# Attention seams in a three-layer hybrid block: order of denominators, first weighting, eviction and reciprocal

## Chip, cores and metric

The kernel runs on one core of a Trainium2 chip. The metric is the device time of one execution in microseconds, as the median of several runs. The core has five engines that work side by side and wait for one another with semaphores: TensorE (PE, matrix products), VectorE (DVE), ScalarE (ACT), GpSimd (POOL) and SyncE (SP, which issues DMAs). Products land in PSUM, eight banks of 128 partitions x 512 fp32.

## What is computed

Input x is (4, 1024, 512) in fp32. Four layers follow one another, each on the layer norm of x and added to x: attention, a top-2 mixture of experts, a state-space mixer, and the experts again. The change is in the attention alone:

```python
kqv = x @ Wqkv + bqkv                              # 16 heads of 32
scores = jnp.einsum('bsnh,btnh->bnst', k, q) / math.sqrt(HEAD_SIZE)
scores = jnp.triu(scores) + -10000.0 * jnp.tril(ones, k=-1)
attn = jax.nn.softmax(scores, axis=2)
out = jnp.einsum('bnkq,bknh->bqnh', attn, v)
out = out.reshape(b, s, NUM_HEADS * HEAD_SIZE)
return out @ Wo + bo
```

## The kernel before

A loop runs over the 4 batches. In the attention of one batch the 16 heads go by pairs: p = 0 to 7, in four groups g of two pairs (hf = 0 and 1). Even pairs are hf 0, odd ones hf 1. During an even pair TensorE also projects queries and keys of the next group (L741 to L743, four parts of 12 matmuls, into PSUM bank 7); the last group has no next one, so pair 6 has no projection. The loop over the groups is split into first, middle and last part, and each engine has its own hand-written order of work; what follows is that order, and each engine keeps strictly to its own.

The scores of a pair are formed twice. Row tiles (`scores_a`, L864 and the mask L867, ten tiles "a" 0 to 9) give the maxima, which VectorE takes (`maximum`, L1586). They are formed one pair ahead. The maxima are turned (`turn_maxima`, L874), cast by ScalarE (L1246) and sent by two DMAs from ScalarE's queue (L1249) into an extra row of QS. Column tiles (`scores_b`, L886 and L889, twelve units u, units 0 to 3 over the first 512 queries and 4 to 11 over the last 512) carry that row, and are then exponentiated by ScalarE into the four buffers of PR (`exponential`, L1263). Three banks of two rotate for all these score tiles, so that a tile waits for the reader of the one three tiles back. Unit 4's scores are the first that wait for the second half of the row of maxima.

On PR three things are done. `weigh` (L906, six times a pair, k = 0 to 5, eight groups of products each) multiplies with the values into bank 6; it waits for the two exponentials of its units, k = 0 also until both halves of the previous pair's outputs are evicted, k = 2 until the first half of its own is. GpSimd adds the units up into `acc` (`sums`, a copy L1922 and ten additions L1913); it starts a pair when the previous pair's denominators are formed, and an exponential waits for GpSimd's reader of its buffer. `denominators` (L916) sums `acc` over partitions with a matrix of ones into bank 7, for the previous pair, right behind the first weighting.

VectorE evicts the outputs (`take`, L1598 to L1601, one half of the queries at a time). ScalarE copies the denominators to `rec` (`take_denominators`, L1270), VectorE inverts them in two halves (`invert`, L1608) and multiplies the outputs (`scale`, L1618, two operations). `rec` is one buffer, so the copy waits for the scaling of the pair before. On VectorE the end of a pair is: first reciprocal of the previous pair, second eviction of this one, second reciprocal, scaling. In an even pair the next thing is `group_lo` (L1622), then the maxima of tiles 0 and 1 and the first eviction of the next pair. The projection of the next group waits on TensorE until the denominators in bank 7 have been copied (den_act). "Seam" means the stretch between the last weighting of a pair and the third weighting of the next.

Of the kernel before, what the change touches and what calls it, by code (L numbers as in the profile page):

```python
# [148 lines left out]
def hybrid_layer(nc, x, Wqkv, bqkv, Wo, bo, W_in, conv_w, conv_b, z_bias, Dskip, W_out,  # L149
                 Wr, br, Wd, bd, Wu, bu, out):  # L150
    with ExitStack() as ctx:
# [108 lines left out]
        pj_lo = signal("pj_lo", 4)  # L260
# [449 lines left out]
        def _(pe):  # L710
# [100 lines left out]
            with pe.Fori(0, NB) as b:  # L811
# [64 lines left out]
                def scores_b(slots, p, q, slot, occ, job):  # L876

                    u = job[1] % UNITS
                    c, s, t0, n = span(u)
                    if s == 0:  # L880
                        pe.wait_ge(s_mrow[slot][c], occ * 32 + 32)
                    slot_free(slots, p, job)
                    bank = slots.bank[job]
                    diag = s * P >= c * HB
                    for hh in range(2):
                        i = pe.matmul(ps[:, bank + hh, 0:n], KS[slot][:, hh, s * P:(s + 1) * P],  # L886
                                      QS[slot][:, hh, t0:t0 + n], start=True, stop=not diag)
                        if diag:
                            i = pe.matmul(ps[:, bank + hh, 0:P], identb[:, :], mask_st[:, :], start=False, stop=True)  # L889
                    i.then_inc(st_pe.sem, 1)  # L890

                def weigh(p, hf, k):

                    ex.wait(pe, p, 2 * k + 2)
                    if k == 0:
                        o_copied.wait(pe, p, 0)
                        vg_done.wait(pe, p, 1)
                    elif k == 2:
                        o_copied.wait(pe, p, 1)
                    for j in range(2):  # L900
                        u = 2 * k + j
                        c, s, t0, n = span(u)
                        at = t0 - c * HB
                        for hh in range(2):
                            h, o = (2 * hf + hh) * HS, j * 64 + hh * HS
                            i = pe.matmul(ps[o:o + HS, 6, at:at + n], VG[:, s, h:h + HS],  # L906
                                          PR[:, u % 4, hh, 0:n], start=(k in (0, 2)), stop=(k in (1, 5)))
                    i.then_inc(pv.sem, 1)

                def denominators(p):  # L910

                    summed.wait(pe, p, 10)
                    for c in range(2):
                        for hh in range(2):
                            o = c * 64 + hh * HS
                            i = pe.matmul(ps[o:o + HS, 7, :], ones[:, 0:HS], acc[:, c, hh, :], start=True, stop=True)  # L916
                    i.then_inc(den_pe.sem, 1)
# [13 lines left out]
                def attend(g, hf, first, last):  # L931
                    p, occ = b * 8 + g * 2 + hf, b * 4 + g
                    close = last and hf == 1
                    slots = SLOTS_CLOSE if close else SLOTS_BODY
                    for k in range(PAIRED):
                        for job in units_of(k):
                            scores_b(slots, p, p, hf, occ, job)
                        weigh(p, hf, k)
                        if k == 0 and not (first and hf == 0):
                            if hf == 1 and not first:  # L940
                                pj_lo.wait(pe, b * 4 + g, 4)
                            denominators(p - 1)
                        if not close:
                            for job in AT[k]:
                                if job[0] == "t":
                                    turn_maxima(slots, p, job[1])
                                else:
                                    scores_a(slots, p, 1 - hf, occ + hf, job[1])
                        if hf == 0 and not last and 1 <= k <= 4:
                            if k == 1 and not first:  # L950
                                den_act.wait(pe, p - 1, 1)
                            project(g + 1, k - 1)
                    if not close:
                        for job in TAIL:
                            if job[0] == "t":
                                turn_maxima(slots, p, job[1])
                            else:
                                scores_b(slots, p, p + 1, 1 - hf, occ + hf, job)

                for part in range(3):  # L960
                    with (pe.Fori(1, GROUPS - 1) if part == 1 else ExitStack()) as i_:
                        g = i_ if part == 1 else (0 if part == 0 else GROUPS - 1)
# [197 lines left out]
        def _(act):  # L1160
# [58 lines left out]
            with act.Fori(0, NB) as b:  # L1219
# [58 lines left out]
                def attend(g, hf, first, last):  # L1278
                    p, occ = b * 8 + g * 2 + hf, b * 4 + g
                    close = last and hf == 1  # L1280
                    slots = SLOTS_CLOSE if close else SLOTS_BODY
                    head = first and hf == 0
                    for u in range(UNITS):
                        exponential(slots if u >= 2 else SLOTS_BODY, ("b", u if u >= 2 else UNITS + u), p, u, head)
                        if u == 1:
                            maxima(SLOTS_BODY, p, 1, hf, None if head else occ - 1 + hf)
                            if hf == 0 and not last:
                                group_hi(b * 4 + g + 1)
                        if u == 3 and not head:
                            take_denominators(p - 1, first and hf == 1)  # L1290
                        if u == 9 and not close:
                            maxima(slots, p + 1, 0, 1 - hf, occ)
                        if hf == 0 and not last and u in (5, 7, 9, 11):
                            project_hi(g + 1, (u - 5) // 2, False)

                for part in range(3):
                    with (act.Fori(1, GROUPS - 1) if part == 1 else ExitStack()) as i_:
                        g = i_ if part == 1 else (0 if part == 0 else GROUPS - 1)
# [114 lines left out]
        def _(dve):  # L1413
# [137 lines left out]
            with dve.Fori(0, NB) as b:  # L1551
# [22 lines left out]
                def project_lo(g, ch, first):  # L1574
                    w, c = ch // 2, ch % 2
                    cols = slice(c * HB, (c + 1) * HB)
                    pj_hi.wait(dve, b * 4 + g, ch + 1)
                    dve.scalar_tensor_tensor(EV[w][1][:, cols], ps[:, 4 + ch if first else 7, :],
                                             bqk[:, w * GROUPS:w * GROUPS + 1] if first else bqk[:, bass.ds(g + w * GROUPS, 1)],
                                             EV[w][0][:, cols].bitcast(F32), ALU.add, ALU.subtract).then_inc(pj_lo.sem, 1)  # L1580
# [9 lines left out]
                def take(p, hf, c, first=False):  # L1590

                    pv.wait(dve, p, 2 if c == 0 else PAIRED)
                    if c == 0 and not first:
                        o_scaled.wait(dve, p - 2, 2)
                    rows_ = slice(c * 64, (c + 1) * 64)
                    f = P if c == 0 else 0
                    if f:
                        dve.tensor_copy(OS[rows_, hf, 0:f], ps[0:64, 6, 0:f])  # L1598
                    dve.tensor_copy(OS[rows_, hf, f:HB], ps[64:128, 6, f:HB]).then_inc(s_half, 1)
                    dve.wait_ge(s_half, p * 2 + (c + 1))  # L1600
                    dve.tensor_tensor(OS[rows_, hf, f:HB], ps[0:64, 6, f:HB], OS[rows_, hf, f:HB], ALU.add).then_inc(o_copied.sem, 1)  # L1601
# [27 lines left out]
                def attend(g, hf, first, last):  # L1629
                    p = b * 8 + g * 2 + hf  # L1630
                    close = last and hf == 1
                    head = first and hf == 0
                    if hf == 0 and not last:
                        group_lo(b * 4 + g + 1)
                    for k in range(1, 5):
                        if not close:
                            for kind, i in AT[k]:
                                if kind == "a":
                                    maximum(SLOTS_BODY, p + 1, i)
                        if k == 1:  # L1640
                            take(p, hf, 0, first)
                        if hf == 0 and not last:
                            project_lo(g + 1, k - 1, False)
                    if not head:
                        invert(p - 1, 0)
                    take(p, hf, 1)
                    if not head:
                        invert(p - 1, 1)
                        scale(p - 1, g if hf == 1 else g - 1, 1 - hf)

                for part in range(3):
                    with (dve.Fori(1, GROUPS - 1) if part == 1 else ExitStack()) as i_:
                        g = i_ if part == 1 else (0 if part == 0 else GROUPS - 1)
# [379 lines left out]
```

## Time and profile before

| | |
|---|---|
| median of 3 runs | 3432.42 us (3430.91 to 3434.16) |
| the profiled execution | 3431.01 us, its span 3429.4 us |
| busy in the span | PE 89%, weight loads 62%, DVE 64%, POOL 35%, ACT 32% |
| mean granted TensorE clock | 0.901 of full speed |
| attention of a batch | from about 187 to 440 us in the first, four times in the span |

The granted clock has two levels, 2.4 GHz (1.00) and 1.2 GHz (0.50); a number between is a mean over a stretch. In the rows, a line of a timeline gives the start in us from the start of the span, the duration of what is merged in it, the engine, line and operation, what it writes and reads, how many, and in square brackets how long the engine had been idle and what ended that. A row of the windows gives a stretch, its length in us, the busy us and number of instructions of PE, PEld, DVE, ACT and POOL in it, the mean granted clock, the busy share of the DMA engines and GB/s. GpSimd's `acc` has the name win_raw there, since it lies in the same memory. The name of TensorE's sequencer or weight load beside it is PEld, and ACTq is ScalarE's sequencer, which issues DMAs.

### The profile page before, as it was taken

Reading aid. Unit: us, or ns where it says so; the run is one execution under the profiler, and the core shown is the slowest. Engines: PE = TensorE matmul, PEld = TensorE weight load, DVE = VectorE, ACT = ScalarE, POOL = GpSimd, SP = SyncE. Lnnn points to the kernel's source line nnn. Section 1 sums busy time; section 2 is a strip of 40 time slices with the busy share of each in tenths; the row PEclk is TensorE's granted clock in tenths of the full one; section 3 lists DMA queues with packets and bytes.
Section 4 is the critical chain, followed back from the end, with each engine's and each line's share of the span. In section 5 each row is a group of like instructions: output and inputs, shape, how many; then the busy total and the mean of one; then the engine's idle time right before and its main releaser. Section 6 shows DMA issues by size and latency. Waiting matters only on the chain.

```text
span 3429.4 us, 59553 instructions
## 1 busy us (share of the span) xinstructions
PE 3043.2 (89%) x19524; PEld 2123.4 (62%) x19524; DVE 2210.9 (64%) x3101; ACT 1104.4 (32%) x1792; POOL 1217.3 (35%) x1341
## 2 busy tenths in 40 slices
PE   3598889999789888999978888899996998899998
PEld 3455457777555446777755444677774554477775
DVE  1356577777645657777764666777764565677776
ACT  1133314444113323344312332343421333144441
POOL 3346511333135541233213553133322455113331
PEclk7779899999879889999988888999998888899998
DMA  7421102111122111111122220111113211021111
GB/s 236 146 55 44 37 19 62 50 48 43 59 69 62 44 25 44 51 48 45 32 81 68 51 48 19 50 43 49 42 42 92 58 44 37 19 62 48 47 46 47
DMA packets 160075, 189.81 MB, mean 55 GB/s; under 512 B 43835, under 2 KB 103867, under 8 KB 158075
## 3 DMA queue, kind: packets, MB, share of 16 engines
q1 hardware_dynamic: 154974, 173.47, 18.2%
q0 software_dynamic: 2720, 10.49, 0.8%
q10 hardware_dynamic: 2176, 3.41, 0.4%
q8 instruction: 94, 1.54, 0.2%
q14 instruction: 111, 0.90, 0.1%
HBM read 104.90 MB, written 23.36 MB: 37 GB/s over the span
## 4 chain that ended last, share of the span: by engine, by line
PE 71%; DVE 10%; issue 5%; POOL 4%; DMA 3%; ACT 2%; SPq 2%; ACTq 1%; POOLq 0%; DVEq 0%
PE ps L741 13%; PE ps L743 12%; PE ps L742 12%; PE ps L864 5%; PE ps L906 5%; PE ps L1084 4%; PE ps L969 3%; POOL win_raw L1913 3%; PE ps L886 3%; PE ps L1070 2%; PE ps L786 2%; PE ps L1130 2%; DVE LM L1713 2%; PE ps L1093 2%; PE ps L751 1%
## 5 line engine op out<-in xcount | busy, mean ns | idle before, releaser
L741 PE MATMUL ps<-uh,win 128*128 128x512 f32 x1536 | 631.3, 411 | 3.5 <-POOL win L1874 2.8
L743 PE MATMUL ps<-uh,win 128*128 128x512 f32 x1536 | 606.7, 395 | 0.0
L742 PE MATMUL ps<-ul,win 128*128 128x512 f32 x1536 | 604.6, 394 | 0.0
L1586 DVE TENSOR_REDUCE mneg<-ps 128x1 f32<-128x640 f32 (+7 forms) x512 | 356.8, 750 | 312.9 <-PE ps L867 311.2
L1913 POOL TENSOR_TENSOR win_raw<-win_raw,PR 128x1024 f32<-128x1024 f32 (+3 forms) x256 | 419.5, 1639 | 191.7 <-ACT PR L1263 130.8
L1263 ACT ACTIVATE PR<-ps 128x1024 f32<-128x1024 f32 (+3 forms) x384 | 292.4, 808 | 357.9 <-PE ps L889 244.5
L1977 POOL TENSOR_SCALAR_AFFINE_SELECT LM<-LM 128x512 f32<-128x512 f32 x256 | 209.6, 830 | 492.4 <-ACT LM L1374 492.4
L741 PEld LDWEIGHTS ps<-uh,win 128*128 128x128 f32 x1536 | 292.3, 190 | 75.7 <-issue 9.5
L864 PE MATMUL ps<-KS,QS 96*128 96x512 f32 (+3 forms) x768 | 278.9, 476 | 67.2 <-DMA KS<-EV 37.2
L743 PEld LDWEIGHTS ps<-uh,win 128*128 128x128 f32 x1536 | 291.7, 190 | 65.9
L1737 DVE TENSOR_TENSOR LM<-ps,LM 128x512 f32<-128x512 f32 x256 | 170.1, 685 | 246.1 <-PE ps L1084 199.5
L742 PEld LDWEIGHTS ps<-ul,win 128*128 128x128 f32 x1536 | 292.8, 191 | 55.1
L886 PE MATMUL ps<-QS,KS 97*128 97x512 f32 (+3 forms) x768 | 272.1, 446 | 28.4 <-ACT PR L1263 21.7
L906 PE MATMUL ps<-PR,VG 128*32 128x512 f32 (+3 forms) x1536 | 219.6, 613 | 56.1 <-DVE OS L1601 52.1
L864 PEld LDWEIGHTS ps<-KS,QS 96*128 96x128 f32 x768 | 166.9, 250 | 143.4 <-issue 57.3
L1725 DVE SCALAR_TENSOR_TENSOR Ct<-ps,cpt,Ct 128x1023 f32<-128x1023 f32 (+2 forms) x192 | 245.5, 1279 | 15.8 <-ACT Ct L1364 11.3
L1725 DVE SCALAR_TENSOR_TENSOR Bt<-ps,cpt,Bt 128x1023 f32<-128x1023 f32 (+2 forms) x192 | 243.4, 1267 | 0.9 <-ACT Bt L1364 0.6
L886 PEld LDWEIGHTS ps<-QS,KS 97*128 97x128 f32 x768 | 163.8, 221 | 108.4 <-issue 53.1
L1184 ACT CAST uh<-ps 128x512 fp32r<-128x512 f32 x128 | 74.0, 588 | 455.7 <-PE ps L751 455.7
L1374 ACT ACTIVATE LM<-ps 128x512 f32<-128x512 f32 x256 | 147.5, 602 | 127.5 <-PE ps L1070 127.5
L1870 POOL TENSOR_TENSOR rstd<-veps,halfs 128x4 f32<-128x4 f32 x32 | 34.4, 1074 | 432.3 <-DVE veps L1447 432.3
L1084 PE MATMUL ps<-Ct,Bt 64*128 64x128 f32 x2048 | 154.2, 292 | 6.1 <-DVE Ct L1725 5.2
(224 smaller groups left out, 5384.4 us busy)
## 6 DMA issues: line engine op xcount, KB each, us to landing
raw<-in_t SPq DMA_DIRECT2D x128, 256.0 KB, 2.7
QS<-EV SPq DMA_DIRECT2D x192, 128.0 KB, 2.3
KS<-EV SPq DMA_DIRECT2D x168, 128.0 KB, 2.4
X<-in_L_attn_b_W_in_dram SPq DMA_DIRECT2D x10, 1024.0 KB, 7.6
in_t<-tiles POOLq DMA_DIRECT2D x10, 1024.0 KB, 7.9
win_raw<-in_L_attn_a_Wqkv_dram SPq DMA_DIRECT2D x34, 256.0 KB, 3.5
X<-in_L_attn_a_x_dram SPq DMA_DIRECT2D x32, 256.0 KB, 4.3
win_raw<-in_t SPq DMA_DIRECT2D x32, 256.0 KB, 2.7
```

The lines of the kernel that those rows point to most:

```text
L741: pe.matmul(dst, hi_l, hi_r, start=first, stop=False)
L742: pe.matmul(dst, hi_l, lo_r, start=False, stop=False)
L743: return pe.matmul(dst, lo_l, hi_r, start=False, stop=last)
L864: w = pe.matmul(ps[:, b0, col:col + m], QS[slot][0:STACK, hh, t * P:(t + 1) * P], KS[slot][0:STACK, hh, c:c + m], start=True, stop=not diag)
L886: i = pe.matmul(ps[:, bank + hh, 0:n], KS[slot][:, hh, s * P:(s + 1) * P], QS[slot][:, hh, t0:t0 + n], start=True, stop=not diag)
L906: i = pe.matmul(ps[o:o + HS, 6, at:at + n], VG[:, s, h:h + HS], PR[:, u % 4, hh, 0:n], start=(k in (0, 2)), stop=(k in (1, 5)))
L1084: i = pe.matmul(ps[:, 5 + h, k * P:(k + 1) * P], Bt[hs, par, tok], Ct[hs, par, tok], start=True, stop=True)
L1263: act.activation(PR[:, u % 4, :, 0:n], ps[:, bank:bank + 2, 0:n], ACT.Exp, scale=SCALE).then_inc(ex.sem, 1)
L1586: m = dve.tensor_reduce(mneg[:, t // HALF, hh, t % HALF:t % HALF + 1], wide(slots.bank["a", i])[:, at:at + (t + 1) * P], AX.X, ALU.max, ne ...
L1725: dve.scalar_tensor_tensor(dst[:, par, k:L], wide(2 * w)[:, 0:L - k], cpt[:, par, w, at:at + 1], dst[:, par, k:L], ALU.mult, ALU.add).then ...
L1913: return pool.tensor_tensor(dst, a, c, ALU.add)
L1977: pool.affine_select(out=v, in_=v, compare_op=ALU.is_ge, fill=0.0, base=0, pattern=[[0, 4], [1, P]], channel_multiplier=-1).then_inc(sel_p ...
```

## The change

Three moves, in the three engines' orders. On TensorE the denominators of the previous pair go ahead of the first weighting instead of behind it. In odd pairs with a projection before them they now wait until that last projection is evicted (before, the wait named the group before, since the weighting's own wait covered it). On ScalarE the copy of the denominators goes behind the exponential of unit 5 instead of unit 3. On VectorE the second eviction goes ahead of both reciprocals instead of between them. No operation is added or taken away.

```diff
                     for k in range(PAIRED):
                         for job in units_of(k):
                             scores_b(slots, p, p, hf, occ, job)
+                        if k == 0 and not (first and hf == 0):
+                            if hf == 1 and not last:
+                                pj_lo.wait(pe, b * 4 + g + 1, 4)
+                            denominators(p - 1)
                         weigh(p, hf, k)
-                        if k == 0 and not (first and hf == 0):
-                            if hf == 1 and not first:
-                                pj_lo.wait(pe, b * 4 + g, 4)
-                            denominators(p - 1)
                         if not close:
@@ -1286,7 +1286,7 @@
-                        if u == 3 and not head:
+                        if u == 5 and not head:
                             take_denominators(p - 1, first and hf == 1)
@@ -1641,10 +1641,9 @@
+                    take(p, hf, 1)
                     if not head:
                         invert(p - 1, 0)
-                    take(p, hf, 1)
-                    if not head:
                         invert(p - 1, 1)
                         scale(p - 1, g if hf == 1 else g - 1, 1 - hf)
```

## Rows read from the trace of the kernel before

**Rows 1.** Part 1 of the page, busy us of each engine:

```profile
PE 3043.2 (89%) x19524; PEld 2123.4 (62%) x19524; DVE 2210.9 (64%) x3101; ACT 1104.4 (32%) x1792; POOL 1217.3 (35%) x1341
```

**Rows 2.** Waits of the whole span: who for whom, us, times, longest:

```profile
ACT PR L1263 <- POOL win_raw L1913: 54.9, 35, 2.8
...
PE ps L906 <- DVE OS L1601: 52.1, 40, 2.0
```

**Rows 3.** Timeline of PE, seam before pair 3, first batch:

```profile
287.05 1.05 PE L906 MATMUL ps<-PR,VG 128*32 128x512 f32 x8 [0.87 <-DVE OS L1601]
287.74 1.23 PE L916 MATMUL ps<-win_raw,ones 128*32 128x512 f32 x8
289.06 1.19 PE L886 MATMUL ps<-QS,KS 97*128 97x512 f32 x4
...
293.17 0.50 PE L864 MATMUL ps<-KS,QS 96*128 96x512 f32 x1 [1.36 <-ACT PR L1263]
...
297.11 1.93 PE L906 MATMUL ps<-PR,VG 128*32 128x512 f32 x8 [1.77 <-DVE OS L1601]
```

**Rows 4.** Timeline of DVE, the same stretch:

```profile
283.07 0.75 DVE L1578 SCALAR_TENSOR_TENSOR EV<-ps,bqk,EV 128x512 fp32r<-128x512 f32 x1 [1.87 <-ACT EV L1237]
283.74 1.74 DVE L1608 RECIPROCAL rec<-rec 128x256 f32<-128x256 f32 x1
...
288.88 1.49 DVE L1618 TENSOR_TENSOR OT<-OS,rec 64x512 f32 x2 [0.18 <-DVE rec L1608]
291.84 1.35 DVE L1586 TENSOR_REDUCE mneg<-ps 128x1 f32<-128x512 f32 x3 [1.46 <-PE ps L867]
294.26 1.35 DVE L1586 TENSOR_REDUCE mneg<-ps 128x1 f32<-128x512 f32 x3 [1.07 <-PE ps L867]
```

**Rows 5.** Timelines of ACT and then of POOL, the same stretch:

```profile
285.85 1.27 ACTq L1249 DMA_DIRECT2D QS<-mrows  x2
...
290.41 0.59 ACT L1270 COPY rec<-ps 128x512 f32<-128x512 f32 x1 [2.15 <-DVE OT L1618]
292.09 1.94 ACT L1263 ACTIVATE PR<-ps 128x1024 f32<-128x1024 f32 x2 [1.09 <-POOL win_raw L1913]
...
279.47 0.74 POOL L1913 TENSOR_TENSOR win_raw<-win_raw,PR 128x256 f32<-128x256 f32 x1 [0.34 <-POOL win_raw L1913]
...
289.33 0.50 POOL L1922 COPY win_raw<-PR 128x256 f32<-128x256 f32 x1 [5.63 <-PE ps L916]
290.01 2.04 POOL L1913 TENSOR_TENSOR win_raw<-PR 128x768 f32<-128x768 f32 x1 [0.18 <-POOL win_raw L1922]
```

**Rows 6.** Timeline of PE, seam before pair 2:

```profile
251.26 1.92 PE L906 MATMUL ps<-PR,VG 128*32 128x512 f32 x8 [1.04 <-DVE OS L1601]
...
258.96 0.49 PE L864 MATMUL ps<-KS,QS 96*128 96x512 f32 x1 [1.72 <-ACT PR L1263]
```

**Rows 7.** Timelines of ACT's queue and of PE, seam before pair 1:

```profile
220.83 1.26 ACTq L1249 DMA_DIRECT2D QS<-mrows  x2
...
224.03 1.18 PE L886 MATMUL ps<-QS,KS 97*128 97x512 f32 x4 [1.03 <-DMA QS<-mrows]
```

**Rows 8.** Windows, ready to ready: pairs 1 (two), 3, 6, 2 and 4:

```profile
221.09:250.22 29.13, 25.28 (x139) 12.78 (x138) 14.56 (x21) 10.22 (x15) 18.11 (x12) 0.82 0.30 72
...
2707.34:2735.25 27.91, 24.02 (x139) 12.47 (x138) 14.56 (x21) 10.22 (x15) 18.13 (x12) 0.88 0.32 77
...
286.18:316.98 30.80, 26.05 (x139) 13.22 (x138) 18.64 (x26) 10.33 (x15) 18.42 (x12) 0.78 0.29 71
...
2869.93:2900.80 30.87, 26.03 (x139) 13.24 (x138) 18.80 (x26) 10.33 (x15) 17.77 (x11) 0.78 0.08 18
...
250.22:286.18 35.96, 32.65 (x186) 19.75 (x186) 22.95 (x31) 13.65 (x20) 18.77 (x12) 0.95 0.20 45
...
2804.75:2839.09 34.34, 31.26 (x186) 19.43 (x186) 24.37 (x31) 13.64 (x20) 19.17 (x12) 1.00 0.20 46
```

**Rows 9.** Timeline of DVE at the end of the first batch's attention:

```profile
437.02 2.36 DVE L1618 TENSOR_TENSOR OT<-OS,rec 64x512 f32<-64x512 f32 x2
```

## The prediction

> **What bounds the kernel now.** I read the busy table first: TensorE works 89% of the span [rows 1], so the other engines matter only where it waits for them. The list of waits comes next. It shows TensorE waiting for the evicted outputs 52.1 us in 40 places, and ScalarE's exponentials waiting for GpSimd's sums 54.9 us in 35 places [rows 2]. The third view is the timeline of one seam, that between head pairs 2 and 3 of the first batch (pairs numbered 0 to 7 in each batch). Four things are to be seen there.
>
> - The first weighting of pair 3 starts at 287.05 after 0.87 us of waiting for L1601, and TensorE was ready at 286.18 [rows 3]. VectorE could have begun the eviction at 283.82, but ran the first half of the reciprocal from 283.74 to 285.48 [rows 4]. This is the queue order that the change turns round.
> - The denominators (L916) stand behind that weighting: 287.74 to 288.97 [rows 3]. GpSimd has had its last sum done since 280.21, and sits idle 5.63 us for the denominators before it copies the next pair's first tile at 289.33 [rows 5].
> - The exponential of unit 4 reuses a buffer of PR that GpSimd's second operation (290.01 to 292.05) reads; it starts at 292.09. The second row-score tile on TensorE (L864 at 293.17) waits 1.36 us for it [rows 3, 5].
> - The third weighting (297.11) waits 1.77 us for the half eviction, which stands behind the maxima of both first tiles (291.84 and 294.26) [rows 3, 4].
>
> So each seam has a wait at the first weighting and one at L864: 1.04 and 1.72 in the seam before pair 2 [rows 6], 0.87 and 1.36 here. The first kind is there in 24 seams (before pairs 2 to 7 of four batches; pair 1 has none), the second weighting wait in 16 pairs (1, 3, 5, 6): together the 40 of [rows 2].
>
> **The change, part by part.**
>
> *Denominators ahead of the weighting.* Same eight matmul passes, 1.23 us [rows 3]. They now run from 286.18 in time that TensorE waited. They need GpSimd's last sum: done 5.97 us before [rows 5]. In odd pairs the wait on the last projection's eviction now asks for the group just projected; behind it on TensorE would stand the denominators and everything after. That eviction ends at 283.82, 2.36 us before [rows 4]. I cost both waits at nothing; if the cover were gone, each us past 286.18 would be a us for TensorE. The denominators end at about 287.4 rather than 288.97, nearly 1.6 us earlier (0.7 for the order, 0.87 for the wait), so GpSimd starts at 287.75, its second operation ends at 290.5, and the exponential of unit 4 ends at 291.5.
>
> *Outputs evicted ahead of the reciprocal.* Two reciprocals of about 1.75 us now follow the eviction. The eviction ends at 285.25, before TensorE is ready: the 0.87 us goes. The scaling still ends near 290.4, since VectorE was never idle from 283.07 to the start of it but for 0.2 us [rows 4]; nothing behind it moves.
>
> *What is late next, odd pairs and pair 6.* Unit 4's scores need the row of maxima that ScalarE sends by DMA. In pair 1, with no wait ahead, they start 1.94 us after the second issue ended at 222.09, and TensorE waits 1.03 us for it [rows 7]. In pair 3 the issues end at 287.12 [rows 5] and the scores start at 289.06 [rows 3], the same 1.94. So this transfer is a bound already, and the 0.87 us turns into a wait for it. The gain comes at L864: ready at 291.81 and released by 291.5, so its 1.36 us go. Behind it VectorE has 1.07 us of idle time between the maxima [rows 4]; with that gone it paces the third weighting, whose wait grows from 1.77 to about 2.0. Net some 1.1 us by this chain alone (1.4 in pair 6).
>
> Pair 1 is the model for what remains: same work, no wait ahead of its first weighting, denominators as well. From ready to ready it lasts 29.13 us in the first batch, 29.19, 29.22 and 27.91 in the others (mean 28.86). The twelve pairs 3, 5 and 6 last 30.07 to 31.96, mean 31.12, at a granted clock of 0.73 to 0.83 against 0.82 to 0.88 [rows 8]. The difference is 2.26 us. I take 2.0, since pair 1 has no reciprocal on VectorE: 12 x 2.0 = 24 us. The bounds are 1.0 (the chain alone, clock as it is) and 3.2 (all as the shortest pair 1).
>
> *Denominators copied two units later, pairs 2 and 4.* ScalarE no longer stops for the scaling ahead of unit 4 (2.15 us before L1270 [rows 5]; it is mostly hidden by GpSimd's sums). But the projection on TensorE waits for the copy, now behind two more exponentials. In pair 2: the two seam waits give 1.04 and some 1.5 us at L864 [rows 6]; unit 4 ends at 256.3, unit 5 at 257.3, the copy (0.59 [rows 5]) at 257.9, so the projection starts at 258.0 rather than 259.83 (L864 at 258.96 plus its 0.87). Gain 1.8 us. In pair 4, at full clock, the row transfer takes away most of the first wait and I get 1.0 us by the same steps. The eight such pairs last 34.34 us at clock 1.00 to 37.66 at 0.91, most 35.9 to 36.0 at 0.95 [rows 8]; some of these low stretches sit right behind the seam's waits. I add 0.6 us for them: 2.0 x 8 = 16 us, bounds 0.7 and 3.3.
>
> *Pair 7.* No row scores. GpSimd adds without a pause for the exponentials to the pair's end, so its earlier start (about 1.7 us) reaches the output projection. I take 1.5 x 4 = 6 us, bounds 0.8 and 1.8.
>
> *Two operands from SBUF.* GpSimd now starts while VectorE scales. At the end of the first batch two scalings beside GpSimd's additions took 2.36 us [rows 9], against 1.49 here [rows 4]; so the two slow each other by up to 0.9 us. I took some 0.3 us a seam off for it above. The Trainium skill (SBUF — State Buffer, on the port pair that DVE and GpSimd share) says that a VectorE operation with two SBUF inputs and a GpSimd operation that reads SBUF exclude each other for the whole instruction. By that rule GpSimd's second operation could be pushed back by both scalings. This is the third case below.
>
> Sum: 24 + 16 + 6 = 46 us off 3431.0, the profiled execution's own time (its span is 3429.4). The median of the runs is 1.4 above that, so 3432.4 - 46 = 3386.
>
> **The rivals.**
>
> 1. *Clock better than that.* The granted clock is below 1.00 in nearly every pair [rows 8], and its fall comes mostly behind the wait at the third weighting (from 297.11 one weighting group takes 1.93 us, against 1.05 at 287.05 [rows 3]). If shorter seam waits kept it up in half of the pairs, another 20 to 30 us go (shortest pair 1: 27.91 at 0.88 [rows 8]): about 3360. Against it: that wait grows a little, and pair 1, which has no other long wait, falls too. Chance 0.13.
>
> 2. *Only the chains, or less.* The clock stays as it is: 12 x 1.1 + 8 x 1.1 + 6 = 28 us, 3404. Pairs 3, 5 and 6 then keep their low stretches although their waits are those of pair 1. Chance 0.17.
>
> 3. *GpSimd held back by VectorE.* If both scalings (1.49 us [rows 4]) run ahead of GpSimd's second operation, unit 4 is no earlier than now. Only the waits at the first weighting go, where the row transfer doesn't take them, some 0.5 us x 24, and pair 7 gains nothing: 12 us, 3420; half of that block gives 3406. For it: [rows 9]. Against it: in [rows 4, 5] a scaling at 288.88 and GpSimd's operations at 289.33 and 290.01 overlap with little loss. Chance 0.08.
>
> 4. *Slower, by the clock.* TensorE's waits move rather than go: onto the row transfer (0.8 us) and the third weighting (2.0). If the clock at 1.2 GHz then lasts longer, work costs up to double while it does. The worst odd pair now (31.96 at 0.73) is 3.1 us over the mean of pair 1, the worst even one (37.66) 3.3 over the best. If every pair fell to these, the 40 us for the pairs would be used up; it decides from there, that is, when each of the 20 pairs is slower than today's worst, and would give about 3440. In [rows 8] the pairs with less waiting have the higher clock, which speaks against. Chance 0.04.
>
> 5. *Nothing.* The waits are handed on whole to the row transfer and the third weighting, 3432. Against it stands pair 1. Chance 0.04.
>
> **How the numbers follow.** Forecast 3386 with chance 0.54, rivals 0.13, 0.17, 0.08, 0.04, 0.04. The range of eight in ten runs from 3356 (first rival) to 3412 (second rival with its lower bounds). 0.2%, or 7 us, is about what a measurement can tell from no change. Faster by more: the first four cases, 0.92. Within: 0.04, the last. Slower: 0.04.
>
> **What would show it.** In the changed kernel: no wait for the eviction ahead of any pair's first weighting; L916 directly ahead of it; GpSimd's first copy some 1.6 us earlier against the scores; the L864 wait under 0.5 us; a wait of 0.5 to 1.0 us for the transfer at unit 4's scores; the third weighting's wait at 1.9 to 2.2; in pairs 2 and 4 a wait under 1 us before the projection; pairs 3, 5 and 6 about 29 us long. The forecast is wrong if L864 still waits over 1 us, if the projection waits for the copy over 2 us, or if the granted clock of pairs 3, 5 and 6 leaves 0.78 to 0.90.

## The result and the profile after

The changed kernel takes 3402.05 us (median of 5 runs, 3392.7 to 3408.44) against 3430.91 (3422.45 to 3434.16) for the kernel before; the ratio is 0.9918, 95% interval 0.9896 to 0.9940. The profiled execution is the shortest of them, 3392.7 us, span 3391.1. Measured again beside the experiments below, on another occasion, the same kernel had 3393.62 us against 3436.88, ratio 0.9883 (0.9841 to 0.9926). So the gain is 0.8 to 1.2%, 29 to 43 us; 46 were forecast.

Where it went is seen in windows from the first weighting of a batch to its last denominators. These are the sums of the four batches, of the kernel before and of the changed one (columns as in [rows 8], without the clock):

```profile
sum 1013.97, PE 889.30 PEld 482.74 DVE 592.64 ACT 357.09 POOL 585.76; mean PE 222.33 PEld 120.68 DVE 148.16 ACT 89.27 POOL 146.44
```

```profile
sum 970.08, PE 860.02 PEld 464.34 DVE 624.49 ACT 358.90 POOL 583.70; mean PE 215.01 PEld 116.08 DVE 156.12 ACT 89.72 POOL 145.93
```

In the repeated profile the sum of the four batches is:

```profile
sum 963.10, PE 852.35 PEld 461.99 DVE 626.12 ACT 359.17 POOL 584.31; mean PE 213.09 PEld 115.50 DVE 156.53 ACT 89.79 POOL 146.08
```

The attention is 43.9 us shorter, the rest of the span 5.6 longer. In the repeated profile it is 50.9 us shorter, the rest 1.6 shorter. The rest has the same instructions; its stretches differ by up to 6 us from one execution to the next, with the granted clock (581.3 us at 0.93 against 575.2 at 0.94). VectorE is 32 us busier with the same operations: that is the first surprise.

The second is how the gain divides. TensorE has the same 1198 instructions in each window, so I read a change of its busy time as the clock's. It falls by 29.3 us in the first profile and by 37.0 in the second; its idle time in the windows, 124.7 us before, falls by 14.6 and 13.9. So two thirds of the gain or more came with the clock. The mean granted clock of a whole execution was 0.897 to 0.910 in the 56 runs of the kernel before that stood beside the experiments, and 0.911 to 0.923 in all eleven of the changed one.

The waits of the changed kernel that answer to [rows 2] (who for whom, us, times, longest), and those for VectorE's `group_lo`:

```profile
ACT PR L1263 <- POOL win_raw L1912: 48.2, 30, 3.1
...
PE ps L906 <- DVE OS L1601: 31.2, 16, 2.0
```

```profile
L1622 DVE TENSOR_TENSOR win<-win_raw,win x12: 1225/1639/1643, 188.9 to 2779.9; 128x1024 fp32r<-128x1024 f32 x12
...
  PEld ps L741: 13.0, 8
  PE ps L741: 11.9, 8
```

All 24 waits ahead of a first weighting are gone; the 16 that are left are those of the third weighting. ScalarE's waits for GpSimd fell little in total, from 54.9 to 48.2 us. The second block (one line's view: durations min/median/max in ns, then who waited for it) shows a wait that the kernel before hadn't: eight first projections wait 1.5 us each for L1622.

The seam before pair 3 again, in the changed kernel. TensorE, to be laid beside [rows 3]:

```profile
284.57 1.06 PE L916 MATMUL ps<-win_raw,ones 128*32 128x512 f32 x8
285.45 1.03 PE L906 MATMUL ps<-PR,VG 128*32 128x512 f32 x8
287.49 1.18 PE L886 MATMUL ps<-QS,KS 97*128 97x512 f32 x4 [1.01 <-DMA QS<-mrows]
...
290.03 0.48 PE L864 MATMUL ps<-KS,QS 96*128 96x512 f32 x1
...
294.77 1.93 PE L906 MATMUL ps<-PR,VG 128*32 128x512 f32 x8 [1.98 <-DVE OS L1601]
```

VectorE, beside [rows 4]:

```profile
283.03 0.68 DVE L1601 TENSOR_TENSOR OS<-ps,OS 64x512 f32<-64x512 f32 x1
283.75 3.37 DVE L1608 RECIPROCAL rec<-rec 128x256 f32<-128x256 f32 x2
287.29 3.34 DVE L1618 TENSOR_TENSOR OT<-OS,rec 64x512 f32 x2 [0.18 <-DVE rec L1608]
290.67 2.61 DVE L1586 TENSOR_REDUCE mneg<-ps 128x1 f32<-128x512 f32 x6
```

ScalarE and GpSimd, beside [rows 5]:

```profile
288.69 1.94 ACT L1263 ACTIVATE PR<-ps 128x1024 f32<-128x1024 f32 x2 [1.99 <-PE ps L886]
290.67 0.59 ACT L1270 COPY rec<-ps 128x512 f32<-128x512 f32 x1
...
285.99 0.40 POOL L1921 COPY win_raw<-PR 128x256 f32<-128x256 f32 x1 [3.83 <-PE ps L916]
286.57 1.82 POOL L1912 TENSOR_TENSOR win_raw<-PR 128x768 f32<-128x768 f32 x1 [0.18 <-POOL win_raw L1921]
288.73 1.35 POOL L1912 TENSOR_TENSOR win_raw<-win_raw,PR 128x512 f32<-128x512 f32 x1 [0.34 <-POOL win_raw L1912]
```

The denominators run where TensorE had waited, GpSimd starts 1.42 us after TensorE is ready (3.15 before), and the exponential of unit 4 is now bound by its scores, not by the sums. L864 doesn't wait. What TensorE waits for instead is the row transfer (1.01) and the third weighting (1.98).

Windows from ready to ready, pairs 1, 2, 3 and 6 of the first batch and pair 6 of the second, beside [rows 8]:

```profile
219.90:249.02 29.12, 25.26 (x139) 12.38 (x139) 14.42 (x22) 10.22 (x15) 18.05 (x12) 0.82 0.30 72
249.02:284.57 35.55, 32.69 (x188) 20.28 (x187) 25.07 (x31) 13.64 (x20) 18.98 (x12) 0.95 0.20 46
284.57:314.01 29.44, 25.19 (x139) 12.37 (x138) 20.28 (x26) 10.44 (x15) 18.23 (x12) 0.83 0.30 74
...
377.48:411.72 34.24, 31.00 (x139) 15.26 (x138) 22.47 (x27) 10.55 (x15) 17.62 (x11) 0.63 0.07 16
...
1201.65:1230.82 29.17, 25.30 (x140) 12.70 (x139) 20.22 (x26) 10.44 (x15) 17.64 (x11) 0.82 0.08 19
```

### The profile page after: what moved, and what is told of

It is laid out like the page before. It is cut to its first block, busy times and chain, and to the rows that moved or that the text cites. A ratio compares the mean times of both kernels' runs of the same rounds, so it can differ in the third digit from the quotient of the medians.

```text
span 3391.1 us, 59557 instructions
## 1 busy us (share of the span) xinstructions
PE 3012.3 (89%) x19524; PEld 2098.0 (62%) x19524; DVE 2243.7 (66%) x3101; ACT 1106.0 (33%) x1792; POOL 1214.1 (36%) x1341
## 4 chain that ended last, share of the span: by engine, by line
PE 70%; DVE 13%; issue 6%; DMA 3%; POOL 3%; SPq 2%; ACT 2%; ACTq 1%; DVEq 0%; POOLq 0%
PE ps L741 13%; PE ps L743 12%; PE ps L742 12%; PE ps L864 5%; PE ps L1084 4%; PE ps L906 4%; PE ps L886 3%; PE ps L969 3%; PE ps L1070 2%; PE ps L786 2%; DVE rec L1608 2%; POOL win_raw L1912 2%; DVE mneg L1586 2%; PE ps L1130 2%; DVE LM L1712 2%
## 5 line engine op out<-in xcount | busy, mean ns | idle before, releaser
L741 PE MATMUL ps<-uh,win 128*128 128x512 f32 x1536 | 631.5, 411 | 12.8 <-DVE win L1622 11.9
L742 PEld LDWEIGHTS ps<-ul,win 128*128 128x128 f32 x1536 | 293.0, 191 | 54.9
L886 PE MATMUL ps<-QS,KS 97*128 97x512 f32 (+3 forms) x768 | 273.8, 444 | 48.6 <-DMA QS<-mrows 22.7
L864 PE MATMUL ps<-KS,QS 96*128 96x512 f32 (+3 forms) x768 | 269.5, 468 | 38.4 <-DMA KS<-EV 38.4
L1724 DVE SCALAR_TENSOR_TENSOR Ct<-ps,cpt,Ct 128x1023 f32<-128x1023 f32 (+2 forms) x192 | 245.5, 1279 | 16.0 <-ACT Ct L1364 11.4
L906 PE MATMUL ps<-PR,VG 128*32 128x512 f32 (+3 forms) x1536 | 206.3, 580 | 41.1 <-DVE OS L1601 31.2
L886 PEld LDWEIGHTS ps<-QS,KS 97*128 97x128 f32 x768 | 161.5, 219 | 131.2 <-issue 68.9
L864 PEld LDWEIGHTS ps<-KS,QS 96*128 96x128 f32 x768 | 163.0, 245 | 108.8 <-issue 55.6
```

Source lines behind the costliest of these rows:

```text
L741: pe.matmul(dst, hi_l, hi_r, start=first, stop=False)
L742: pe.matmul(dst, hi_l, lo_r, start=False, stop=False)
L864: w = pe.matmul(ps[:, b0, col:col + m], QS[slot][0:STACK, hh, t * P:(t + 1) * P], KS[slot][0:STACK, hh, c:c + m], start=True, stop=not diag)
L1724: dve.scalar_tensor_tensor(dst[:, par, k:L], wide(2 * w)[:, 0:L - k], cpt[:, par, w, at:at + 1], dst[:, par, k:L], ALU.mult, ALU.add).then ...
```

## The experiments

Theory A was mine of the prediction: GpSimd's earlier start carries the gain, and the copy was mostly hidden. Theory B: the moves hang together, since an earlier GpSimd lengthens VectorE's scaling, and a copy left behind unit 3 then waits for it. Theory C, which comes up for one kernel, is that the copy alone carries the gain. The times are medians of 5 to 12 runs. "Attention" is the sum of the four windows above, in the one profiled execution. It moves with the clock too: the windows of the four first pairs, in which none of the moves acts, add up to 127.3 to 137.9 us in these profiles, so a difference of a few us between two sums shows nothing.

| kernel | time, us | before, us | ratio (95%) | attention, us |
|---|---|---|---|---|
| before | | 3430.9 to 3436.9 | 1 | 1014.0 |
| TensorE's order alone | 3447.5 | 3432.5 | 1.0043 (1.0018 to 1.0068) | 1026.3 |
| VectorE's order alone | 3434.2 | 3432.5 | 1.0007 (0.9990 to 1.0023) | 1002.6 |
| ScalarE's copy alone | 3434.1 | 3436.9 | 1.0002 (0.9976 to 1.0027) | 1021.1 |
| all but the copy | 3447.6 | 3432.5 | 1.0048 (1.0032 to 1.0064) | 1030.0 |
| all but VectorE's order | 3388.9 | 3432.5 | 0.9877 (0.9855 to 0.9898) | 961.3 |
| the change, again | 3393.6 | 3436.9 | 0.9883 (0.9841 to 0.9926) | 963.1 |

**TensorE's order alone.** The edit of `attend` on TensorE as in the change, nothing else.

> Only TensorE's order is changed (denominators ahead of the first weighting); ScalarE's copy stays behind unit 3, VectorE's eviction between the reciprocals. Theory A (the gain comes from GpSimd's earlier start): the first weighting doesn't wait any more, L1922 starts 1.5 us earlier against the scores, L864's wait goes, and some 30 of the 44 us of the attention are gained. Theory B (the chain needs the copy out of ScalarE's way): the scaling on VectorE now meets GpSimd's additions and ends 1 us later, ScalarE's copy behind unit 3 waits for it, the exponential of unit 4 starts no earlier than before, L864 still waits 1 to 2 us: attention 0 to 12 us shorter than before.

The attention is 12.3 us longer than before. The seam before pair 3, TensorE, VectorE, ScalarE and GpSimd:

```profile
294.24 0.50 PE L864 MATMUL ps<-KS,QS 96*128 96x512 f32 x1 [1.71 <-ACT PR L1263]
...
289.36 3.28 DVE L1618 TENSOR_TENSOR OT<-OS,rec 64x512 f32 x2 [0.18 <-DVE rec L1608]
...
292.68 0.59 ACT L1270 COPY rec<-ps 128x512 f32<-128x512 f32 x1 [3.94 <-DVE OT L1618]
293.16 1.95 ACT L1263 ACTIVATE PR<-ps 128x1024 f32<-128x1024 f32 x2
...
288.60 1.81 POOL L1913 TENSOR_TENSOR win_raw<-PR 128x768 f32<-128x768 f32 x1 [0.18 <-POOL win_raw L1922]
```

GpSimd's second operation ended at 290.41, but ScalarE stood 3.94 us in the copy, for scalings of 3.28 us that took 1.49 before [rows 4]. Theory B, and more of it than I had written: not even the small gain is left.

**VectorE's order alone.**

> Only VectorE's order is changed. Both theories: no wait ahead of the first weighting, so the denominators behind it come 0.9 to 1.0 us earlier. Theory A: all of this reaches L864, 24 x 0.9 = 22 us less in the attention. Theory B: ScalarE's copy waits for a scaling that ends where it did or later, the exponential of unit 4 moves by less than 0.5 us, attention 5 to 12 us shorter. The first projection of pairs 2 and 4 waits for L1622 in neither.

Time unchanged. The attention is 11.4 us shorter in the profile, which looks like what theory B gave, but 8.7 of it lies in pairs 0 and 1, whose windows the edit doesn't touch and which ran at a higher clock; pairs 2 to 6 together are 0.7 us shorter. The profiled execution was also 9 us below the median of its kernel. So the move gained next to nothing in its own seams, less than theory B's 5 to 12. ScalarE's copy waits 98.2 us in 26 places for the scaling, against 34.2 in 16 before.

**All but the copy.**

```diff
-                        if u == 5 and not head:
+                        if u == 3 and not head:
                             take_denominators(p - 1, first and hf == 1)
```

> The changed kernel with ScalarE's copy put back behind unit 3. Theory A: within 8 us of the changed kernel (the copy was hidden by GpSimd's sums). Theory B: the copy waits some 3 us for scalings that take 3.3 us beside GpSimd's additions, the exponential of unit 4 is 2 us later than in the changed kernel, and L864 waits 1.5 to 2 us again: attention 20 to 30 us longer than with the change.

1030.0 us of attention, 60 more than with the change, twice what I gave theory B. An edit of one number turns a gain of 1% into a loss of 0.5%.

**All but VectorE's order.**

> The changed kernel with VectorE's eviction back between the reciprocals. The denominators already fill the time that TensorE waits for the eviction, so the first weighting should not wait. Theory A and B: within 8 us of the changed kernel, either side, since the row transfer bounds unit 4's scores; the scaling is as late, since VectorE has the same work in the seam. A rival (the eviction order carries the gain): 15 us or more slower than the changed kernel, with a wait for L1601 ahead of the first weighting.

3388.9 us and 961.3 us of attention: no worse than the change. The eviction ahead of the reciprocals is worth nothing once the denominators fill the time that TensorE had waited for it; the rival is out.

**ScalarE's copy alone.**

```diff
-                        if u == 3 and not head:
+                        if u == 5 and not head:
                             take_denominators(p - 1, first and hf == 1)
```

> Only ScalarE's copy is moved, from behind unit 3 to behind unit 5. Theory B (the copy matters only once GpSimd starts earlier): the exponential of unit 4 is bound by GpSimd's sums as before, L864 waits 1.3 to 1.7 us as before, the first projection of pairs 2 and 4 starts 0.5 to 1 us later: attention from 5 us shorter to 8 us longer than before, time within 0.3%. Theory C (the copy alone carries the gain): 20 us or more faster.

Same time, attention 7 us longer; theory C is out. Each of the three moves alone gives nothing or a loss, and TensorE's and ScalarE's together give all of it.

**Two buffers for the denominators.** TensorE's order alone, with `rec` doubled (the second one lies in a buffer of the layer norm that is idle here), and the copy still behind unit 3. The lines on the copy; the reciprocals and the scaling take the same buffer by its number:

```diff
                     if not first:
-                        o_scaled.wait(act, p - 1, 2)
+                        o_scaled.wait(act, p - 2, 2)
-                    act.copy(rec[:, :], ps[:, 7, :]).then_inc(den_act.sem, 1)
+                    act.copy(rec[i], ps[:, 7, :]).then_inc(den_act.sem, 1)
```

> TensorE's order as in the change, VectorE's and ScalarE's as before, but two buffers for the denominators, so that the copy behind unit 3 no longer waits for the scaling of the pair before. Theory B: what made TensorE's move alone slower was this one wait; without it the exponential of unit 4 starts 2.5 us earlier, and the attention is as short as with the copy moved (955 to 970 us), perhaps 3 us shorter because the projection is released sooner. A rival (the scalings that GpSimd's additions lengthen hold TensorE up by another way): over 1000 us.

3392.5 us, ratio 0.9879 (0.9844 to 0.9913), attention 970.0. VectorE is as busy as with TensorE's order alone (632 us against 634), so the scalings are as long; only the wait for them is gone. So it was this one wait that turned TensorE's move into a loss.

**GpSimd held back until the scaling is done.**

```diff
                         until(den_pe, p - 1, 1)
+                        until(o_scaled, p - 2, 2)
```

> The changed kernel, but GpSimd begins a pair's sums only when VectorE's scaling of the pair before last is done, so that the two don't run side by side there. If the long scalings come from the two engines meeting: the median of L1618 falls from 1.64 to 0.69 us, the two together from 3.3 to 1.4. The sums start some 3 us later, so the exponential of unit 4 waits for them and the attention gets longer again, 990 to 1030 us. If they come from something else, L1618 stays above 1.2 us.

3470.2 us, ratio 1.0109 (1.0083 to 1.0134), attention 1043.5, above the 990 to 1030 that I gave it. L1618 in the change, and here, and the seam before pair 3 here, VectorE and GpSimd:

```profile
L1618 DVE TENSOR_TENSOR OT<-OS,rec x64: 682/1638/1669, 251.8 to 2894.5; 64x512 f32<-64x512 f32 x32, 64x512 f32 x32
```

```profile
L1618 DVE TENSOR_TENSOR OT<-OS,rec x64: 682/686/1100, 252.0 to 2973.8; 64x512 f32<-64x512 f32 x32, 64x512 f32 x32
...
290.39 1.41 DVE L1618 TENSOR_TENSOR OT<-OS,rec 64x512 f32 x2 [0.18 <-DVE rec L1608]
...
292.13 0.40 POOL L1922 COPY win_raw<-PR 128x256 f32<-128x256 f32 x1 [6.87 <-DVE OT L1618]
```

With GpSimd out of the way the scaling takes 0.69 us instead of 1.64. The meeting of the two engines is shown, and so is its price: 0.95 us for each of two scalings, on VectorE. GpSimd's first addition hardly changes (1.82 beside the scalings, 1.80 without). The Trainium skill (SBUF — State Buffer, "Who interferes with whom") says that a VectorE instruction with two SBUF inputs contends with a GpSimd instruction that reads SBUF, and that who issues first keeps the shared pair for the whole instruction. The trace agrees: GpSimd's addition began at 286.57, the scaling at 287.29, and the scaling paid. The addition of 288.73 ended at 290.08, and the second scaling, which had begun at 288.97, ended 0.55 us after that, at 290.63. In the kernel before, the first scaling came first, at 288.88, and GpSimd paid most of what little there was: its copy took 0.50 us and its addition 2.04 [rows 5], against 0.40 and 1.80 here.

**`group_lo` ahead of the scaling.** At the seam before pairs 2 and 4, L1622 goes before L1618.

> The changed kernel with L1622 ahead of the scaling on VectorE at the seams before pairs 2 and 4. The wait of the first projection for L1622 (1.5 us in 8 places) goes; the copy of the denominators, which now waits for a scaling 1.6 us later, takes its place: the projection starts within 0.5 us of where it does now, and the attention is within 8 us of the changed kernel's. If L1622 alone had held it: 8 x 1.5 = 12 us shorter.

3386.2 us, ratio 0.9884 (0.9845 to 0.9922): the same time as the change; attention 975.1, with pairs 2 and 4 together 7 to 9 us longer than in the change. The wait for L1622 is gone and this one is there in its place:

```profile
PE ps L741 <- ACT rec L1270: 17.9, 8, 2.3
```

It is 2.3 us at most, longer than the 1.5 it replaces. The first projection hangs on the copy and on L1622, and both queue behind VectorE's 3.3 us.

**The first eviction between the maxima.** The change, and on VectorE, in all pairs but the last of a batch:

```diff
                                 if kind == "a":
                                     maximum(SLOTS_BODY, p + 1, i)
-                        if k == 1:
+                                if kind == "a" and i == 0:
+                                    take(p, hf, 0, first)
+                        if k == 1 and close:
                             take(p, hf, 0, first)
```

> The changed kernel with the first eviction between the maxima of tiles 0 and 1. The third weighting waits 0.7 us instead of 2.0 in 16 pairs; 16 x 1.3 = 21 us less in the attention (940 to 955), and a little more if the granted clock of the odd pairs rises with it. If the maxima of tile 1 then hold up tile 2: a new wait for L1586 of 1 us and half of that gain.

3327.85 us, ratio 0.9697 (0.9672 to 0.9723): by the two ratios another 64 us off the change, from moving one call. The attention lasts 901.4 us, 62 less than in the change's repeated profile, where I gave 21. TensorE before pair 3, and the windows of pairs 1 and 3:

```profile
286.73 1.94 PE L906 MATMUL ps<-PR,VG 128*32 128x512 f32 x8 [0.70 <-DVE OS L1601]
```

```profile
219.46:243.67 24.21, 21.28 (x139) 10.78 (x138) 14.33 (x22) 10.17 (x15) 18.13 (x12) 1.00 0.37 89
277.78:303.70 25.92, 22.81 (x139) 11.38 (x139) 20.19 (x26) 10.37 (x15) 18.28 (x12) 0.93 0.35 83
```

The wait is 0.70, as expected. Of the 62 us only 13 are idle time of TensorE; 49 are busy time of the same instructions, so most came with the clock. In pair 1 of the first batch the third weighting waits 1.3 us less (1.97 to 0.72), but the pair falls from 29.12 us at clock 0.82 to 24.21 at 1.00, 4.9 us, and TensorE's busy time alone from 25.26 to 21.28. The changed kernel has one such pair at full clock: pair 1 of the fourth batch in its repeated profile, with the wait still at 1.97.

```profile
2679.07:2704.36 25.29, 21.24 (x139) 10.78 (x138) 14.33 (x22) 10.17 (x15) 18.14 (x12) 1.00 0.35 85
```

Against it the shorter wait gives 1.1 us, and the other 3.8 are the clock. The slow stretch behind the third weighting was the dearest thing in the pair.

With waits of 0.62 to 0.72 the clock stayed at 1.00 in 12 of the 16 pairs 1, 3, 5 and 6 and fell in 4, the pair 3 shown here among them (its weighting takes 1.94 us, half speed); with 1.88 to 1.98 it fell in 31 of 32, over both profiles of the changed kernel. So the shorter wait makes the fall rarer; it doesn't rule it out, and the longer one doesn't always bring it. What decides in a single pair is open.

**Reciprocals out of the seam, twice.** Both start from the kernel above, with the copy behind unit 3. In the first, reciprocals stand behind tile 1 and the scaling behind tiles 2 to 4; in the second the reciprocals are parted.

```diff
+                        if k == 1 and not head:
+                            invert(p - 1, 0)
+                            invert(p - 1, 1)
+                        if k == 2 and not head:
+                            scale(p - 1, g if hf == 1 else g - 1, 1 - hf)
                     take(p, hf, 1)
-                    if not head:
-                        invert(p - 1, 0)
-                        invert(p - 1, 1)
-                        scale(p - 1, g if hf == 1 else g - 1, 1 - hf)
```

> TensorE's order as in the change; on VectorE both reciprocals and the scaling leave the seam: the first eviction goes between the maxima of the first two tiles, the reciprocals behind them, the scaling behind tiles 2 to 4, where VectorE was idle; ScalarE's copy behind unit 3, where it then waits for nothing. If VectorE's queue in the seam is what bounds now: the third weighting waits 0.7 us instead of 2.0 in 16 pairs, the first projection doesn't wait for L1622, the attention lasts 915 to 940 us and the time is 3335 to 3365. If the clock eats it: 3370 or more.

3365.35 us, ratio 0.9802 (0.9768 to 0.9836), at the upper end of what I gave; attention 949.2, above it. TensorE, in pair 3, and VectorE in the seam before it:

```profile
291.19 1.06 PE L906 MATMUL ps<-PR,VG 128*32 128x512 f32 x8 [0.71 <-DVE OS L1601]
296.63 0.80 PE L886 MATMUL ps<-QS,KS 97*128 97x512 f32 x1 [2.26 <-DVE mneg L1586]
...
288.34 1.35 DVE L1586 TENSOR_REDUCE mneg<-ps 128x1 f32<-128x512 f32 x3 [6.48 <-PE ps L867]
```

The third weighting waits 0.71, as hoped, but 2.26 us have moved to the next tiles' maxima, behind the two reciprocals, and the clock is low behind them (one L886 product takes 0.80 us, against 0.50 at full clock). This wait is there in all 16 pairs.

> As spread_u3, with the reciprocals parted: the first behind the maxima of tile 1, the second behind those of tiles 2 to 4, the scaling behind the next. In spread_u3 both stand ahead of tiles 2 to 4 and TensorE waits 2.26 us for those maxima (L886 at 296.63). If that wait is on the path: it falls under 1 us in 12 pairs and the time is 3345 to 3362. If it only moves to tiles 5 to 9: as spread_u3, 3360 to 3370.

3340.9 us, ratio 0.9722 (0.9697 to 0.9747), attention 913.8, a little better than either case that I gave. The wait of 2.26 us is 0.65 now in all 16 pairs, and a second one of 0.5 to 1.7 us for later maxima has come behind it, so it is in part removed and in part moved. It is still not as good as leaving the reciprocals in the seam (3327.85). With them out, VectorE stands idle 6.48 us there until tile 0's scores come (the line at 288.34 above). In the kernel with the eviction between the maxima they and the scaling take 6.9 us, nearly that time, from 276.96 to 283.85:

```profile
276.96 3.36 DVE L1608 RECIPROCAL rec<-rec 128x256 f32<-128x256 f32 x2
280.51 3.34 DVE L1618 TENSOR_TENSOR OT<-OS,rec 64x512 f32 x2 [0.18 <-DVE rec L1608]
283.88 1.35 DVE L1586 TENSOR_REDUCE mneg<-ps 128x1 f32<-128x512 f32 x3
```

The seam only looked like the crowded place.

## Why the prediction was right, and where not

- **Sum.** The attention is 44 us shorter in one profile and 51 in the other, against 46; the median fell by 29 in one comparison and 43 in the other. That the sum comes so near is in part luck. Rival 2 puts 28 us of the 46 down to the waits, which leaves 18 for the clock. The runs showed 14 to 15 us of idle time and 29 to 37 of busy time: the waits gave half of what they were priced at, the clock half as much again or twice, and the two errors cancelled. Rival 2 itself (the clock unchanged, 3404) is what the first median looks like, but not how it came about: the granted clock in the attention of a batch was 0.84 to 0.86 before, 0.86 to 0.90 with the change, and 0.87 to 0.94 in its repeated profile. (Its sum takes 1.1 us for pairs 2 and 4, whose chains are put at 1.8 and 1.0 above it; with their mean of 1.4 it is 30.) Up to 4 us of the attention's gain lie in pairs 0 and 1, in which no move acts.
- **Denominators ahead.** Right: no wait for GpSimd's last sum in any seam, none for the last projection's eviction, GpSimd earlier. TensorE ran the eight products in 0.88 us of its time (284.57 to 285.45).
- **Row transfer and third weighting.** Right to 0.1 us: 1.01 and 1.98 against "0.5 to 1.0" and "1.9 to 2.2". L864's wait is gone.
- **Pairs 3, 5, 6 become as pair 1.** Right for most in length: 29.15 to 29.5 us in eight of twelve, 26.97 to 34.24 over all. One pair 6 stayed at half clock for most of its 34.24 us; with it the twelve give 20.4 us where 24 were forecast, and 29.9 in the repeated profile. The way there differs. In pair 3 of the first batch TensorE's idle time falls by 0.5 us (30.80 - 26.05 to 29.44 - 25.19), where the chain had 1.1, and its busy time by 0.9. One of the forecast's own signs of being wrong came true as well: the granted clock of these pairs left 0.78 to 0.90 in four of twelve (0.63, 0.77 and twice 0.94), and was 0.94 in four of twelve in the repeated profile. Pair 7 gave 7.9 against 6.
- **Pairs 2 and 4.** Failed in part: 11.9 us in one profile, 10.2 in the other, against 16, and most of it is the clock's. Where that is alike, at 0.95, the pairs took 35.91 to 35.99 us before and 35.55 to 35.70 after; at 1.00 they took 34.34 and 34.09 to 34.11. So the shorter waits are worth 0.2 to 0.4 us a pair, where the chains were put at 1.8 and 1.0; the rest comes of five pairs of eight at full clock, against one before. The failed step is "the scaling still ends near 290.4", so that "nothing behind it moves". In the seam before pair 2 of the changed kernel, VectorE, then TensorE, and last TensorE's projection in the kernel before:

```profile
251.77 3.33 DVE L1618 TENSOR_TENSOR OT<-OS,rec 64x512 f32<-64x512 f32 x2
255.13 1.64 DVE L1622 TENSOR_TENSOR win<-win_raw,win 128x1024 fp32r<-128x1024 f32 x1
...
256.82 0.80 PE L741 MATMUL ps<-uh,win 128*128 128x512 f32 x1 [1.60 <-DVE win L1622]
257.42 0.63 PE L742 MATMUL ps<-ul,win 128*128 128x512 f32 x1
...
260.15 0.39 PE L742 MATMUL ps<-ul,win 128*128 128x512 f32 x1
```

  The projection does start 7.80 us after TensorE is ready, as forecast (258.0 - 250.22), but behind a wait of 1.60 us, and in all eight pairs that wait is 1.4 to 1.6 where "under 1 us" was forecast. Behind it the first seven products run at half clock (0.63 us against 0.39), and the block of twelve takes 4.3 us here (256.82 to 261.14) against 2.9 before (259.83 to 262.68). I had named the copy as what the projection waits for, and overlooked `group_lo`, which stands behind the scaling on VectorE. [rows 9] had shown the meeting of the two engines, and I read it as both slowing each other: of its 2.36 us the first scaling takes 0.68 and the second 1.64, so one scaling alone was held up, by 0.96. I took 0.3 us a seam for it, the same 0.26 us that I had already taken off because pair 1 has no reciprocal, and it is 1.9 on VectorE. The rival that I made of it had the wrong engine pay: GpSimd was held back by no more than 0.1 us an addition.
- **The copy.** Wrong in kind, though the sum hid it. I wrote that its wait was mostly hidden by GpSimd's sums, which was true of the kernel before alone. Without that move the other two lose 0.5%. The wait that one edit lengthens has to be looked for in the state that the other edits leave.
- **Eviction ahead of the reciprocal.** I had this end the first wait; the denominators alone end it, and I counted one wait as removed by two edits.

## What to carry to other kernels

Price a set of moves as a set: an engine that starts earlier meets others in new places, and here a copy left where it was turned the gain into a loss. When a wait is bounded by an engine's queue, look through that queue for a short operation that others need and that stands behind a long one that is needed later; this was worth 64 us, more than the change. And price a wait on TensorE with the clock behind it, and set busy time beside idle time to tell the two apart: in pair 1 the shorter wait gave back 1.1 us and the clock 3.8.

## What the runs showed of the hardware

- Two scalings with both operands in SBUF took 3.3 us beside GpSimd's additions and 1.4 alone; GpSimd's additions beside them took 1.82 against 1.80, so the delay fell on VectorE. Where a scaling began first, GpSimd's operation paid, with 0.1 to 0.2 us (0.50 against 0.40, 2.04 against 1.80).
- Pairs with a wait of TensorE of 1.88 to 1.98 us had a granted clock of 0.82 or 0.83 mostly (0.63 to 0.94 in 31 of 32, 1.00 in one); with 0.62 to 0.72 it was 1.00 in 12 of 16, and 0.82 to 0.93 in four. Pair 1, always the same instructions, took 29.12 us at 0.82 (first batch), 25.29 at 1.00 with the same wait (fourth batch, repeated profile), and 24.21 at 1.00 with the shorter one.
- The transfer of the maxima (two DMAs of 2 KB from ScalarE's queue) let TensorE go 1.9 us after the second issue ended, before (224.03 after 222.09) and after the change alike (287.49 after 285.58), and is what now bounds unit 4's scores.
